# Self-attention: the next quarter's maxima over ten of twelve steps, and their row one step later

## What is computed

```python
K = jnp.einsum('bse,hed->bhsd', xk, Wk)
V = jnp.einsum('bse,hed->bhsd', xv, Wv)
Q = jnp.einsum('bqe,hed->bhqd', xq, Wq)
scores = jnp.einsum('bhqd,bhkd->bhqk', Q, K)
if masked:
    causal = jnp.triu(jnp.ones((xq.shape[1], sk), dtype=bool), k=1)
    scores = jnp.where(causal, -jnp.inf, scores)
att = jax.nn.softmax(scores / jnp.sqrt(jnp.asarray(sk, scores.dtype)), axis=-1)
out = jnp.einsum('bhqk,bhkd->bhqd', att, V)
```

## Time and profile before

| what | value |
|---|---|
| time, median of 3 runs | 2992.64 us (2990.46 to 2996.18) |
| time of the profiled execution | 2986.63 us |
| its span, first to last instruction | 2984.8 us |
| mean granted TensorE clock | 0.926 of full |
| TensorE matmul busy | 2539.0 us (85%) |
| VectorE busy | 1596.2 us (53%) |
| ScalarE busy | 1293.5 us (43%) |
| GpSimd busy | 1208.6 us (40%) |
| the 384 reductions L3053 | 347.1 us busy |
| the 768 exponentials L2974 | 353.9 us busy |
| self-attention, first unit to last values | about 1142 to 1902 us of the span |

### The profile page before, as it was taken

The page is one execution under the profiler, slowest core; times in us unless marked ns, Lnnn a source line. Parts: engine busy times, 40 slices in busy tenths (PEclk is TensorE's granted clock), DMA queues, the critical chain, the costliest instruction groups (busy, mean ns, idle before and its releaser), DMA issues. The chain is left out here.

```text
span 2984.8 us, 43672 instructions
## 1 busy us (share of the span) xinstructions
PE 2539.0 (85%) x13250; PEld 1486.1 (50%) x13251; DVE 1596.2 (53%) x3227; ACT 1293.5 (43%) x2566; POOL 1208.6 (40%) x1717
## 2 busy tenths in 40 slices
PE   7997999999947748888888989599949885899997
PEld 4554667666625533343343343256534574466664
DVE  5884656555538736647556656288836535222211
ACT  4663435344337714545445546356642232222221
POOL 3665651344437730120210210136880352566663
PEclk9998999999979977999999999899979865899999
DMA  4001000001000031221221311000002331222222
GB/s 124 5 1 61 0 0 1 1 1 43 1 32 1 0 76 42 51 58 45 51 63 38 76 42 33 22 29 22 1 26 87 131 109 45 39 46 46 46 45 30
DMA packets 86053, 117.22 MB, mean 39 GB/s; under 512 B 13864, under 2 KB 64144, under 8 KB 84080
## 3 DMA queue, kind: packets, MB, share of 16 engines
q1 hardware_dynamic: 68944, 96.01, 11.1%
q0 software_dynamic: 16928, 18.93, 4.0%
HBM read 80.00 MB, written 34.64 MB: 38 GB/s over the span
## 5 line engine op out<-in xcount | busy, mean ns | idle before, releaser
L2974 ACT ACTIVATE L2S_pT<-L2S_t_ps 128x512 f32<-128x512 f32 (+3 forms) x768 | 353.9, 490 | 237.1 <-PE L2S_t_ps L2872 127.3
L3053 DVE TENSOR_REDUCE L2S_mx<-L2S_s_ps 128x1 f32<-128x768 f32 (+7 forms) x384 | 347.1, 952 | 111.1 <-PE L2S_s_ps L2851 107.6
L2869 PE MATMUL L2S_t_ps<-L2S_q,L2S_k 98*128 98x512 bf16 (+3 forms) x768 | 251.9, 342 | 40.8 <-ACT L2S_pT L2974 33.3
L2850 PE MATMUL L2S_s_ps<-L2S_k,L2S_q 96*128 96x512 bf16 (+3 forms) x768 | 208.5, 344 | 43.9 <-DVE L2S_mx L3053 32.7
L3158 POOL DMA_DIRECT2D L2S_q<-L2S_mrow x32 | 17.2, 538 | 431.3 <-DVE L2S_mrow L3061 431.2
L3512 DVE TENSOR_TENSOR L3B_h<-L3B_si,L3B_u_ps 128x512 f32<-128x512 f32 x71 | 48.8, 687 | 237.0 <-PE L3B_u_ps L3455 237.0
L571 POOL TENSOR_TENSOR L_prob<-L_prob,L_rc 128x616 f32<-128x616 f32 x64 | 77.8, 1215 | 234.9 <-DVE L_rc L524 234.9
L2869 PEld LDWEIGHTS L2S_t_ps<-L2S_q,L2S_k 98*128 98x128 bf16 x768 | 75.6, 99 | 191.5 <-ACT L2S_pT L2974 146.7
L3429 POOL DMA_INDIRECT out<-L3B_y,L3F_rows x71 | 114.7, 1616 | 134.8 <-DVE L3B_y L3518 120.2
L2887 PE MATMUL L2S_o_ps<-L2S_pT,L2S_v 128*32 128x512 f32 (+3 forms) x1536 | 167.1, 510 | 0.0
L310 PE MATMUL L_scores<-weights,L_xT 128*128 128x308 f32 x512 | 143.1, 423 | 2.2 <-ACT L_xT L426 1.6
(11 more groups left out here) (493 smaller groups left out, 5929.6 us busy)
## 6 DMA issues: line engine op xcount, KB each, us to landing
qk_parts<-L2S_part SPq DMA_DIRECT2D x96, 128.0 KB, 2.3
L2S_q<-qk_parts SPq DMA_DIRECT2D x32, 192.0 KB, 3.5
L2S_k<-qk_parts SPq DMA_DIRECT2D x32, 192.0 KB, 3.5
L2S_q<-qk_parts SPq DMA_DIRECT2D x32, 128.0 KB, 3.2
L2S_k<-qk_parts SPq DMA_DIRECT2D x32, 128.0 KB, 3.3
self_attended<-L2S_att SPq DMA_DIRECT2D x4, 1024.0 KB, 4.3
L_xn<-self_attended SPq DMA_DIRECT2D x8, 512.0 KB, 3.5
L2F_wgu<-in_L_gu SPq DMA_DIRECT2D x8, 512.0 KB, 8.1
```

Source lines behind the costliest of these rows:

```text
L2850: nc.tensor.matmul(o[:, z * 512 + c:z * 512 + e], lhs, k6[0:KR, q % 2, h, c:e], start=True, stop=(e < end))
L2869: mm = nc.tensor.matmul(o[:, lo:512], k6[:, q % 2, j, kt * P:(kt + 1) * P], q6[:, q % 2, j, c * 512 + lo:(c + 1) * 512], start=True, stop= ...
L2974: nc.scalar.activation(pT[:, st % 2, j, lo:512], t_ps[j % 2][:, lo:512], ACT.Exp, scale=SK).then_inc(s["exp_done"], 1)
L3053: nc.vector.tensor_reduce(dst, src, AX.X, ALU.max).then_inc(s["mx_done"], 1)
```

## The change

Two constants of `self_stage` change. The peaks of the next quarter stand in other steps, still in the same order and with the same total of 24; and `turn_max`, on TensorE, VectorE and GpSimd alike, stands in step 10, where it stood in step 9.

```diff
-    SHARE = ((0, 0, 0, 2, 7, 5, 4, 3, 3, 0, 0, 0), (3, 2, 1, 2, 4, 4, 3, 3, 2, 0, 0, 0))
-    TURN_AT = 9
+    SHARE = ((0, 0, 0, 2, 6, 4, 3, 3, 3, 3, 0, 0), (3, 2, 1, 1, 3, 3, 3, 3, 3, 2, 0, 0))
+    TURN_AT = 10
```

## The result

The changed kernel takes 3020.09 us (median of 4 runs, 3017.74 to 3024.76) against 2991.55 us for the kernel before (4 runs, 2990.33 to 2996.18): a ratio of 1.0098, 95% interval 1.008 to 1.0117, **28.5 us slower**. The forecast was 3005, its range ended at 3016. The profiled execution took 3018.61 us, with a span of 3016.6.

A forecast was written before the change was run, and what follows sets the result against it. Prediction: TensorE's quarter starts are bound by the row of maxima arriving, a taut 3.94 us path. 10.9 + 1.0 + 6.0 - 5.2 - 4.0 + 4.0 = +12.7 us, forecast 3005 on the medians' scale, range 2994 to 3016.

The forecast's parts named there:

- the late landing: Row's two GpSimd transfers, now among SP's loads at six quarter starts, land later than the 1.8 us median: +1, bound 7.2.
- the clock at the six starts: New TensorE stalls at six quarter starts bring the granted clock down, three falls taken of six: +4.0 us, between 0 and 8.0.
- Rival 2: Every stall at the six starts brings the clock down and the transfers land late: +24.9, 3017.5 us; chance 0.12 with beyond +20.
- The row at six starts: Row of maxima transposed a step later; only step 11 hides it at six quarter starts, 3.82 us each: +10.9 us.
- The last maxima behind the normalisation: Second quarter, first three batches: two 1024-wide reductions behind VectorE's normalisation delay TensorE's transposes, +2.0 us three times: +6.0 us.
- Rival 4: Reductions behind the normalisation cost nothing, as TensorE waits there anyway: +6.7, 2999.3 us; within the 0.62 for +6 to +20.
- Spreading: Maxima moved to emptier steps shorten four first quarters by 5.2 us in all and eight later ones by 4.0.
- All other starts at nothing: Nine other quarter starts have a projection or batch end, 7 us and more, hiding the later row: costed at nothing.

The follow-up runs named there:

- the filler: Changed kernel plus six unused fp32 matmuls (four at the last start) before TensorE's wait for the row of maxima at six quarter starts; 3008.41 us, ratio 1.0062.

## Why the prediction was off in size

The direction, the mechanism and every place that it named were right; it gave +12.7 us and the medians say +28.5. Two terms of its sum were mis-sized above all: the late landing (+1 for a measured +6.9) and the clock at the six starts (+4.0 for +8.6). Rival 2 (+24.9) came nearest, with the same mechanisms at larger sizes. Step by step:

1. **The row at six starts, +10.9: right.** With the loads out of the way the last steps took 22.66 us, 10.6 more than before.
2. **Late landing, +1 (bound 7.2): mis-sized, it measured +6.9.** This is the step that failed first. The prediction saw that the transfers move past SP's loads and then took a value near the lower bound, "the packets are few and small". In the microseconds in question the DMA engines were 79 to 85% busy. The row's landing without neighbours was the wrong row to be near to. The upper bound of 7.2 came close by luck: it rests on the slowest landing before, 3.0 us, and that one stood beside an instruction packet; SP's packets began only 0.1 us before it landed (1832.59 and 1832.70). The Trainium skill, page "DMA: Bandwidth & Descriptors", section "Anatomy of one DMA — SWDGE (gpsimd) path", gives about 2.0 us fixed; the landings of 1.7 to 2.1 us with the loads behind the row agree, the 3.4 us among the loads is not in it.
3. **The clock, +4.0 for three falls of six: mis-sized, it measured +8.6 at these places,** which the filler shows (35.60 with it, 44.20 without). All six stalls brought it down, at up to 2.4 us each (8.39 against 5.96). At 1.34 each, six falls had been put at 8.0; the count was the error. It didn't hang on the late landing: stalls of at most 2.2 us did it as well. The rule of the Trainium skill's page "TensorE: Matmul & The Clock Gate", section "HAM oscillation — how this bites in real kernels", would have let the clock stand behind those; here it fell behind six of six, and the measurement decides. In the four kernels with the late row and no filler the clock fell behind all 24 stalls, in the two with a filler behind none of 12.
4. **The last maxima behind the normalisation, +6.0: right in itself.** Steps 3 to 10 grew by 5.9 us in the three batches (7.0 in step 10, less 1.1 in steps 3 to 9). Rival 4 falls with the wait of 7.17 us in place of 4.84. A further 1.9 is once more a fall of the clock, in the third batch's step 11, which the term didn't have.
5. **Spreading, -5.2 and -4.0.** The first is right (-5.6). The later quarters gave 0.39 us each in steps 3 to 9 (23.88 to 23.49) and lost 0.09 of it in step 10, -2.4 in all. What was off is steps 3 and 4, which were to be 0.6 shorter and went from 5.55 to 5.39 us. There was little to get: TensorE's wait for reductions was 0.7 us a quarter.
6. **"All other starts at nothing": right.** The list of waits has no wait for the row beyond the six starts and the stage's first unit, and the last steps ahead of the nine others take what they took (9.38 and 2.4 us, 21.4), but for the clock's fall in one.
7. **What nobody's term held.** The stage comes to +24.3 and the medians to +28.5. In the profiled executions the time from the stage's last step on was 1084.7 us before and 1090.2 after. In the ten experiments, whose code is the same there, it was 1081.7 to 1085.3 us in seven and 1087.8 to 1090.8 in three. Those three are the executions that lay 5.2 to 5.5 us above the median of their own kernel, so this stretch seems to differ between executions of one kernel, and the changed kernel's profiled execution, with 1090.2, still lay 1.5 us under its median. With one profile of each kernel it isn't shown where the 4.2 us come from; this stays open. So does what sets how long a fall lasts.

The stage alone, with +24.3, already lies past the +23.4 with which the range ended, and the rest of the +28.5 took the time further, to 3020. Rival 2's sum, +24.9, is nearly the stage's; it had been given 0.12, because two terms on which no row of before decided were put low and in the middle.

## What to carry to other kernels

A small transfer whose arrival starts the next phase has to be costed with what is on the DMA engines at its new time, not with its median landing; if another queue's bulk loads begin there, hold them back or issue the small one first. Before reductions are moved to an emptier step, look at what stands ahead of them on their own in-order engine, not only at that engine's idle share there. And a stall of TensorE of 2 us beside sparse matmuls should be costed with its fall of the clock; the wait that was longest before (here the normalisation's, 4.84 us three times) was worth more than any spreading of the maxima.

## What the runs showed of the hardware

- An 8 KB transfer by GpSimd's queue lands in 1.7 to 2.1 us alone and in up to 3.6 us when six loads of SP's queue are issued in the same 4 us (five starts, some 1.4 us each; 85% DMA share, 222 GB/s). Beside a single packet of an instruction queue it took up to 3.0 us in the kernel before, at a DMA share of 0.06 to 0.08.
- Matmuls of no use in a stall kept the granted clock at 2.4 GHz at 12 of 12 starts, where it fell at 24 of 24 without them. Behind the wait for the normalisation, falls came in none to three of the three second quarters, depending on the kernel (step 11 at 9.37 to 9.42 us, or at 10.90 to 11.37 with a fall). In the sparse last quarter a fall once stood for most of 37 us (0.68 on the mean, 6.4 us lost).
- The time of the later stages, whose code is the same in all kernels, went from 1081.7 to 1090.8 us between one kernel's profile and the next; what it is, no run shows.
